# One slot in every 64 fetched by SyncE, row by row, in place of a GpSimd gather

## The chip, the cores and the metric

The kernel runs on one core of a Trainium2 chip. The metric is the device time of one execution in microseconds (us): the median of several timed runs. All inputs and outputs are in HBM.

## What is computed

A graph network over N = 6250 nodes with 128 features and E = 200000 edges, which are sorted by destination. Two attention layers and one message layer each read the row of every edge's source node:

```python
# attention layer (twice), heads H=8, C=16
xs = (x @ lin_w.T).reshape(N, H, C)
alpha = a_src[src] + a_dst[dst] + a_edge
alpha = leaky_relu(alpha); m = segment_max(alpha, dst)
alpha = exp(alpha - m[dst]); alpha /= segment_sum(alpha, dst)[dst]
out = segment_sum(xs[src] * alpha[..., None], dst)
...
# message layer
em = relu(layer_norm(concat([x[src], x[dst]]) @ msg_w + msg_b))
msgs = segment_sum(em * edge_weights[:, None], dst)
```

Everything else (projections, layer norms, the update at the end) works on nodes, not on edges, and is short.

## The kernel before

**Tiling.** The edges are cut into slots of 128 edges whose destinations lie in one block of 128 nodes. There are 1616 slots. Four slots (G = 4) make a visit, so there are 404 visits (VISITS), and eight visits (SPAN) make a group z of the softmax. An edge's source row is fetched from a table in HBM into a ring in SBUF. Such a fetch is an indirect DMA of GpSimd: one instruction for each slot, 128 rows at once, addressed by a column of the index tile `slot_src`.

**Stages.** There are three stages with such gathers, one after another, each over all visits. Pass 1 reads `rows1` (265 floats a row, 1060 bytes) into a ring of 5 visits. Pass 2 reads `rows2` (136 floats) into a ring of 24 visits. The message stage reads `msg_rows` (128 floats) into a ring of 4 visits, and fetches 1624 slots. Node work lies between the stages.

**Order in a pass.** Each engine has its own hand-written program over a counter t, and semaphores join them. In iteration t of a pass:

- GpSimd (`edge_rows_in`) gathers visit v once visit v - 5 of the ring is consumed (pass 1) and once PE has selected the destinations of visit v - 4 (LEAD).
- ACT (`edge_act`) copies the part xs of visit t out of the ring (pass 1 alone, L1163), then evacuates the transposed one-hot of visit t + 2 (L1169), then casts the one-hot of visit t - 15 (L1175), and then does its step of the softmax.
- PE selects destination rows of visit t + 1 (L1073) and scatters visit t - 16 (L1057 to L1060).
- DVE takes the scores of visit t from the ring (`edge_take`, L1280 to L1285), weights, makes the one-hots (L1249) and adds.

The softmax of group z runs in steps p = 0 to 7 at t = 8 + 8z + p. In pass 1 its step 2 ends with an ACT copy that signals `e2_out` (L1203), which is at t = 8z + 10; step 5 is ACT's exp (L1211); DVE signals `topped` in step 5 or so (L1362).

**SyncE's queue.** In a pass SyncE issues few transfers (`edge_side_loads`). For each z it waits for `topped` of z - 2, issues three small loads (L995, L997, L998; in pass 2 a fourth, L1000), and in pass 1 then waits for `e2_out` of group z - 1 and stores that tile (L1004). In the message stage it issues nothing until the very end.

Of the kernel before, what the change touches and what calls it, by code (L numbers as in the profile page):

```python
# [41 lines left out]
SPAN = 8  # L42
WS = SPAN * G
# [47 lines left out]
class Build:  # L91


    def __init__(self, nc, ctx):
# [4 lines left out]
        self.arrived_before = [0] * ROWS_MOST  # L99

# [79 lines left out]
def load(queue, relay, dst, src):  # L180

    relay.done(queue.dma_start(dst, src))
# [12 lines left out]
class Setup:  # L195
# [3 lines left out]
    def __init__(self, K, edges):  # L199
# [42 lines left out]
        self.dstf = K.sb("lane_keys", [P, SC, P])[:, :, :]  # L242
# [13 lines left out]
def prepare(K, D, edges):  # L256
# [10 lines left out]
    erows = Relay(K.arrived[ROWS_MOST - 1], 16)  # L267
# [106 lines left out]
    srcs.done(act.activation(T.srcf, T.erow[:, :, 0, :].bitcast(i32), ACT.Copy))  # L374
    turned = K.relay("slots_turned")
# [51 lines left out]
    for relay in (made, filled, cleared, fold, place, srcs, words, wts, turned, evacuated, copied, squared, multiplied, copied_a,  # L427
                  links_out, wt_out, sent, h0_out, keys_first):
        relay.after(pe, act, dve, sp)
# [235 lines left out]
def project(K, name, sources, width, evacuate):  # L665

    pe, act, dve = K.pe, K.act, K.dve  # L670
    transposed, copied = K.relay(name + "_transposed"), K.relay(name + "_copied")
    multiplied, evacuated = K.relay(name + "_multiplied"), K.relay(name + "_evacuated")
    units = [(b, k) for b in range(NB) for k in range(len(sources))]

    def transpose(q):
        b, k = units[q]
        if q >= 2:
            pe.wait_ge(copied.sem, q - 1)
        transposed.done(pe.transpose(K.ps[:, q % 2, 0:P], sources[k][0][:, b, :], K.ident[:, :]))
        act.wait_ge(transposed.sem, q + 1)  # L680
        if q >= 2:
            act.wait_ge(multiplied.sem, q - 1)
        copied.done(act.activation(K.xT[:, q % 2, :], K.ps[:, q % 2, 0:P], ACT.Copy))

    transpose(0)
    for q, (b, k) in enumerate(units):
        if q + 1 < len(units):
            transpose(q + 1)
        pe.wait_ge(copied.sem, q + 1)
        if k == 0 and b >= 2:  # L690
            pe.wait_ge(evacuated.sem, b - 1)
        multiplied.done(pe.matmul(K.ps[:, 2 + b % 2, 0:width], K.xT[:, q % 2, :], sources[k][1],
                                  start=k == 0, stop=k == len(sources) - 1))
        if k == len(sources) - 1:
            dve.wait_ge(multiplied.sem, q + 1)
            evacuated.done(evacuate(b, K.ps[:, 2 + b % 2, 0:width]))
# [26 lines left out]
class DmaEvent:  # L723


    def __init__(self, K, sems, each, before):
        self.K, self.sems, self.each, self.before = K, sems, 16 * each, before
# [4 lines left out]
    def wait(self, engine, i, v):  # L732
        self.K.loop_wait(engine, self.at(v), i, self.each, (v // U + 1) * self.each + self.before[v % U])
# [10 lines left out]
class Gather:  # L744


    def __init__(self, K, name, source, buffer, freed, extra):
        self.K, self.source, self.buffer, self.freed = K, source, buffer, freed
        self.arrived = DmaEvent(K, K.arrived, G, list(K.arrived_before))
        for u in range(U):  # L750
            K.arrived_before[u] += 16 * G * (TURNS + (1 if u < extra else 0))

    def emit(self, i, v):
# [3 lines left out]
        for j in range(G):  # L757
# [58 lines left out]

WITHIN = "a slot's block counts the 48 block starts passed, and moves by one at most from slot to slot"
# [42 lines left out]
class Pass:  # L860


    def __init__(self, K, layer):
# [52 lines left out]
        event = lambda what: K.sem(n + what)  # L916
        self.made, self.transposed, self.turned, self.selected = event("made"), event("transposed"), event("turned"), event("selected")
        self.consumed, self.xs_copied, self.cast, self.columns = event("consumed"), event("xs_copied"), event("cast"), event("columns")
# [1487 lines left out]
```

## Time and profile before

| What | us |
|---|---|
| Median of 3 timed runs | 8398.62 (8397.52 to 8403.86) |
| Span of the profiled execution, first to last instruction | 6747.1 |
| Pass 1, gathers, from about | 92 to 2132 |
| Pass 2, gathers, from about | 2315 to 4349 |
| Message stage, to about | 6600 |

Of the profiled execution only the span is given, and no time of its own; the median of the timed runs is 1651.5 us above that span. The profile shows nothing outside the span. All rows below belong to the span. The two passes and the message stage make up nearly all of it.

### The profile page before, as it was taken

The page shows a single profiled execution, that of the slowest core. Times are in us where ns is not written, and L with a number is a line of the kernel's source. Part 1 is how long each engine was busy: PE and PEld are TensorE (multiplying, and loading weights), DVE is VectorE, ACT ScalarE, POOL GpSimd, SP SyncE. Part 2 cuts the span into 40 slices and gives each one's busy share as a digit, 9 for nine tenths or more (in the row PEclk, how much of TensorE's full clock was granted, in tenths as well). Part 3 has the DMA queues.
Part 4 walks back from the last instruction along what each step waited for, and adds up shares of the span by engine and source line. Part 5 has one row for each costly group of instructions (what it writes and reads, how often), then busy time and mean ns, then how long its engine had stood idle before and what let it go on. Part 6 is the DMA issues. An engine that isn't in the chain of part 4 may idle for free. (4 is left out here: it accounts for less than half of the span.)

```text
span 6747.1 us, 141313 instructions
## 1 busy us (share of the span) xinstructions
PE 5205.8 (77%) x33770; PEld 4594.2 (68%) x33770; DVE 4667.0 (69%) x15724; ACT 3002.7 (45%) x10366; POOL 4638.6 (69%) x4899
## 2 busy tenths in 40 slices
PE   4888888888888289989898988866776667767664
PEld 4667667677766277878787877756666666666664
DVE  4777777777777656666666666566777777777777
ACT  2444444444443322222222222265666666666666
POOL 4777777777774277777777777506777777777771
PEclk6898998989998666666666666678999999999997
DMA  7544444444443422222222222232222222222222
GB/s 168 152 117 116 116 116 116 117 116 116 116 116 77 115 62 63 62 63 65 63 63 63 63 64 63 49 87 60 54 54 54 54 54 54 54 54 54 54 54 30
DMA packets 335610, 537.84 MB, mean 80 GB/s; under 512 B 105870, under 2 KB 223135, under 8 KB 334481
## 3 DMA queue, kind: packets, MB, share of 16 engines
q0 software_dynamic: 182080, 441.08, 26.1%
q1 hardware_dynamic: 143462, 83.65, 4.6%
q8 instruction: 357, 5.85, 0.4%
q10 hardware_dynamic: 9323, 4.08, 0.3%
q14 instruction: 388, 3.18, 0.2%
HBM read 491.47 MB, written 42.61 MB: 79 GB/s over the span
## 5 line engine op out<-in xcount | busy, mean ns | idle before, releaser
L976 POOL DMA_INDIRECT arena<-rows,slot_src x3232 | 3081.1, 953 | 1024.2 <-issue 910.8
L759 POOL DMA_INDIRECT arena<-msg_rows,slot_src x1624 | 1532.5, 944 | 494.7 <-issue 489.4
L2071 PE MATMUL psum<-arena 128*128 x3248 | 710.1, 303 | 585.7 <-DVE arena L2091 364.6
L1169 ACT ACTIVATE arena<-psum 128x512 f32<-128x512 bf16 x808 | 479.9, 594 | 1305.0 <-PE psum L1018 1294.5
L2071 PEld LDWEIGHTS psum<-arena 128*128 128x128 f32 x3248 | 526.8, 204 | 655.0 <-issue 654.7
L1305 DVE TENSOR_TENSOR arena<-arena,psum 128x290 f32 x1616 | 731.4, 453 | 323.3 <-DVE arena L1305 312.9
L1058 PE MATMUL psum<-arena 128*128 128x145 f32 x3232 | 954.5, 386 | 0.0
L1073 PE MATMUL psum<-arena 128*128 x3232 | 687.7, 343 | 262.8 <-DVE arena L1285 157.0
L1060 PE MATMUL psum<-arena 128*128 128x145 f32 x3232 | 881.7, 364 | 0.0
L1437 DVE TENSOR_TENSOR arena<-arena,psum 128x129 f32 x1616 | 468.8, 290 | 528.6 <-PE psum L2132 465.0
L1073 PEld LDWEIGHTS psum<-arena 128*128 128x128 f32 x3232 | 518.0, 211 | 393.3 <-issue 365.5
L1073 PE MATMUL psum<-a_src_a_dst,arena 128*128 x3232 | 637.8, 316 | 177.3 <-DVE arena L1285 138.4
L2078 ACT ACTIVATE arena<-psum 128x128 bf16<-128x128 f32 x1624 | 426.1, 277 | 772.6 <-PE psum L2073 772.3
L1073 PEld LDWEIGHTS psum<-a_src_a_dst,arena 128*128 128x128 f32 x3232 | 608.0, 269 | 231.1 <-issue 219.1
L1060 PEld LDWEIGHTS psum<-arena 128*128 128x128 f32 x3232 | 675.3, 250 | 10.5 <-issue 2.4
L1242 DVE TENSOR_TENSOR arena<-arena,psum 128x512 f32<-128x512 f32 x808 | 553.5, 685 | 180.9 <-PE psum L1060 177.8
L2073 PE MATMUL psum<-arena,ident 128*128 128x128 f32 x3248 | 675.7, 292 | 0.0
L1058 PEld LDWEIGHTS psum<-arena 128*128 128x128 f32 x3232 | 643.8, 247 | 44.6
L2091 DVE SCALAR_TENSOR_TENSOR arena<-psum,node_small,vectors 128x128 f32<-128x128 f32 x1620 | 561.0, 346 | 44.4 <-DVE node_small L2087 1.8
L1249 DVE TENSOR_TENSOR arena<-psum,slot_local_dst 128x512 bf16<-128x512 bf16 x808 | 551.7, 683 | 0.2
L1280 DVE CUSTOM_DVE_ANT_0 arena<-arena,psum 128x128 bf16<-128x128 f32 x1616 | 367.8, 282 | 253.4 <-DMA arena<-rows,slot_src 185.4
L2073 PEld LDWEIGHTS psum<-arena,ident 128*128 128x128 f32 x3248 | 536.8, 208 | 0.0
(361 smaller groups left out, 9250.5 us busy)
## 6 DMA issues: line engine op xcount, KB each, us to landing
arena<-rows,slot_src POOLq DMA_INDIRECT x3232
arena<-msg_rows,slot_src POOLq DMA_INDIRECT x1624
arena<-slot_keys SPq DMA_DIRECT2D x100, 128.0 KB
edge_alpha<-arena SPq DMA_DIRECT2D x50, 128.0 KB
arena<-edge_alpha SPq DMA_DIRECT2D x50, 128.0 KB
slot_keys<-lane_keys SPq DMA_DIRECT2D x24, 256.0 KB
arena<-rows SPq DMA_DIRECT2D x6, 1024.0 KB, 9.9
rows<-arena SPq DMA_DIRECT2D x4, 822.0 KB
```

What stands on the lines that cost most here:

```text
L759: pool.indirect_dma_start(out=self.buffer[:, v % U, j, :], out_offset=None, in_=self.source, in_offset=bass.IndirectOffsetOnAxis(ap=K.SRC[ ...
L976: pool.indirect_dma_start(out=E.rowbuf[:, r, j, :], out_offset=None, in_=E.source, in_offset=bass.IndirectOffsetOnAxis(ap=K.SRC[:, at:at + ...
L1058: pe.matmul(sums[:, 0:AW], E.onehotF[:, u % 2, 2 * k, :], E.rhs[:, u % 2, 2 * k, :], start=True, stop=False, skip_group_check=True)
L1060: pe.matmul(K.ps[:, 3 + k, bass.ds(step_in(word, k), AW)], E.onehotF[:, u % 2, 2 * k + 1, :], E.rhs[:, u % 2, 2 * k + 1, :], start=False, ...
L1073: return pe.matmul(E.psX[:, j, 0:E.dcol], E.onehotT[:, v % 2, j, :], rows_.rearrange("p b w -> p (b w)"), start=True, stop=True)
L1169: act.activation(E.onehotT[:, v % 2, :, :], E.psT, ACT.Copy).then_inc(E.turned, 1)
L1242: dve.tensor_tensor(by_head(E.rhs[:, u % 2, :, 0:F]), by_head(xs), w.unsqueeze(3).broadcast_to([P, G, H, C]), ALU.mult).then_inc(E.weighte ...
L1249: dve.tensor_tensor(E.onehot[:, v % ONEHOTS, :, :], E.iota.unsqueeze(1).broadcast_to([P, G, P]), K.DL[:, v * G:v * G + G].unsqueeze(2).bro ...
L1305: dve.tensor_tensor(row, row, E.psB(k), ALU.add).then_inc(E.added, 1)
L2071: pe.matmul(psH[b][:, j, :], onehotT[:, b, j, :], K.by_dst[:, bass.ds(blocks(v, j), 1), :].rearrange("p b w -> p (b w)"), start=True, stop ...
L2073: last = pe.matmul(psH[b][:, j, :], K.ident[:, :], rowbuf[:, b, j, :], start=False, stop=True)
L2091: last = dve.scalar_tensor_tensor(rhs[:, b, j, 0:F], psH[b][:, j, :], rstd[:, b, j:j + 1], K.vec["L1_gnn_msg_g"], ALU.mult, ALU.mult)
```

## The change

One slot of every 64 is taken from GpSimd: slot j = 0 of each visit v = 15, 31, 47 and so on to 399 (`ASIDE`), 25 visits; in pass 1 the first two are left as they were, so there are 23. SyncE fetches the 128 rows of such a slot with 128 transfers of one row each. It reads the indices eight at a time from SBUF into registers; for each row it computes the address and issues the transfer into a staging buffer of two slots (which lies in the `lane_keys` tile). ScalarE then copies the 128 staged rows into the ring, one iteration ahead of the visit's first reader, and all readers of such a visit wait for that copy too. In the passes SyncE issues 64 rows after its side loads of each z, and so a slot in two halves (z even, z odd). In the message stage it issues them all in one sequence. The list of indices is kept in HBM once, in the setup.

```diff
+EVERY = 2 * SPAN
+ASIDE = [v for v in range(EVERY - 1, VISITS, EVERY)]
+IDX = 8
...
+    def load_indices(self, n):
...
+        sp.dma_start(K.aside_idx[:, n % 2, :], K.aside_src[i % 2:i % 2 + 1, i // 2, :]).then_inc(K.aside_idx_in[n % 2], 16)
+
+    def gather(self, n, part, parts):
+        K, sp = self.K, self.K.sp
+        if part == 0:
+            if n == 0:
+                self.load_indices(0)
+            sp.wait_ge(K.aside_idx_in[n % 2], self.idx_landed[n])
+            if n + 1 < len(self.visits):
+                self.load_indices(n + 1)
+            at_least(sp, self.copied, n - 1)
+        for at in range(part * P // parts, (part + 1) * P // parts, IDX):
+            _, nodes = K.nc.values_load_multi_w_load_instructions(K.aside_idx[0:1, n % 2, at:at + IDX], engines=[ET.SP],
+                                                                  skip_runtime_bounds_check_because=NODES)
+            for k in range(IDX):
+                node = nodes[k].with_bounds(min_val=0, max_val=N - 1)
+                sp.dma_start(self.buffer[at + k:at + k + 1, n % 2, :], self.source[bass.ds(node, 1), :]
+                             ).then_inc(K.aside_in[n % IDX], 16)
+
+    def copy(self, n, to):
+        K, act = self.K, self.K.act
+        act.wait_ge(K.aside_in[n % IDX], self.landed[n])
+        act.activation(to, self.buffer[:, n % 2, :], ACT.Copy).then_inc(self.copied, 1)
...
     def wait_rows(self, engine, v):
         r = v % self.rows
-        engine.wait_ge(self.K.arrived[r], self.before[r] + (v // self.rows + 1) * 16 * G)
+        engine.wait_ge(self.K.arrived[r], self.before[r] + sum(16 * len(js) for js in self.by_pool[r:v + 1:self.rows]))
+        n = self.aside.of(v)
+        if n is not None:
+            engine.wait_ge(self.aside.copied, n + 1)
...
         r = v % E.rows
-        for j in range(G):
+        for j in E.by_pool[v]:
...
             sp.wait_ge(E.e2_out, z)
             sp.dma_start(K.edge2[z - 1, :, 0:w], E.e2[:, b, 0:w]).then_inc(E.kept[b], 16)
+        n = E.aside.of(z // 2 * EVERY + EVERY - 1)
+        if n is not None:
+            E.aside.gather(n, z % 2, 2)
...
     for t in range(-2, VISITS + 16):
+        n = E.aside.of(t + 1)
+        if n is not None:
+            at_least(act, E.consumed, t + 2 - E.rows)
+            if not E.first:
+                at_least(act, E.weighted, t + 2 - E.rows)
+            E.aside.copy(n, E.rowbuf[:, (t + 1) % E.rows, 0, :])
...
+    S.sent.after(sp)
+    for n in range(len(gather.aside.visits)):
+        gather.aside.gather(n, 0, 1)
...
+        n = gather.aside.of(i * U + v + 1)
+        if n is not None:
+            summed.wait(act, i, v + 1 - U)
+            gather.aside.copy(n, rowbuf[:, (v + 1) % U, 0, :])
```

SyncE's queue in pass 1, at two neighbouring z, before (L1004 is the store that waits for `e2_out`):

```order
L997 DMA arena<-slot_keys 128x1
L998 DMA arena<-chunk_links 1x66
L1004 DMA edge_alpha<-arena 128x256 [waits edge1_e2_out]
L995 DMA arena<-slot_keys 128x2x128 [waits edge1_topped]
L997 DMA arena<-slot_keys 128x1
```

and the same place now, for an odd z, where the second half of a slot begins (L1033 to L1042 are the lines L995 to L1004 of before; L710 reads eight indices, the ISA row computes an address, L714 fetches one row of `rows1`):

```order
L1033 DMA arena<-slot_keys 128x2x128 [waits edge1_topped]
L1035 DMA arena<-slot_keys 128x1
L1036 DMA arena<-chunk_links 1x66
L1042 DMA edge_alpha<-arena 128x256 [waits edge1_e2_out]
L710 TENSOR_LOAD aside_indices
L714 ISA
L714 DMA lane_keys<-rows 1x265
L714 ISA
L714 DMA lane_keys<-rows 1x265
```

Behind the last of these rows the pair of ISA and DMA goes on to 64 rows, with a L710 before every eight; then comes the next z's L1033. So 64 transfers now stand between a store and the next side loads, and behind the wait for `e2_out`.

ACT's program in pass 1 around the first visit taken aside (v = 47), now; L1258 is the exp (L1211 before), L1210 the copy of xs (L1163), L1216 the evacuation of the one-hot (L1169), and L721 is new:

```order
L1222 ACTIVATE arena<-arena 128x512 [waits edge1_scattered]
L1224 ACTIVATE arena<-arena 128x4x16 [waits edge1_wt_out]
L1258 ACTIVATE arena<-arena 128x256 [waits edge1_lowered]
L721 ACTIVATE arena<-lane_keys 128x265 [waits aside_rows_in0,edge1_consumed]
L1210 ACTIVATE arena<-arena 128x512 [waits edge1_weighted,rows_arrived1]
L1216 ACTIVATE arena<-psum 128x512 [waits edge1_selected,edge1_transposed]
```

The copy of visit 8z + 7 (z odd) stands at the head of iteration t = 8z + 6, behind the exp of the softmax and ahead of everything else that ACT does from there on. The `e2_out` for which SyncE waits before the second half is signalled at t = 8z + 2, three iterations and a softmax step earlier.

## Rows read from the trace of the kernel before

**Rows 1.** The page: busy time of each engine over the span.

```profile
span 6747.1 us, 141313 instructions
PE 5205.8 (77%) x33770; PEld 4594.2 (68%) x33770; DVE 4667.0 (69%) x15724; ACT 3002.7 (45%) x10366; POOL 4638.6 (69%) x4899
```

**Rows 2.** Windows in pass 1, pass 2, message stage: busy us (instructions), clock, DMA share, GB/s.

```profile
core 0: us, PE busy (x) PEld busy (x) DVE busy (x) ACT busy (x) POOL busy (x), PEclk, DMA share, GB/s
1000.00:1500.00 500.00, 423.74 (x2697) 354.10 (x2697) 394.97 (x1724) 220.15 (x552) 378.44 (x400) 0.91 0.43 116
3000.00:3500.00 500.00, 450.39 (x2515) 401.46 (x2514) 304.73 (x729) 143.67 (x363) 378.91 (x398) 0.66 0.27 63
5000.00:5500.00 500.00, 342.57 (x2808) 321.02 (x2807) 361.86 (x1129) 308.61 (x1400) 378.11 (x401) 0.96 0.21 54
```

**Rows 3.** Groups of instructions, POOL: busy us, mean ns, idle before, releasers.

```profile
L976 POOL DMA_INDIRECT arena<-rows,slot_src x3232 | 3081.1, 953 | 1024.2 <-issue 910.8 <-PE psum L1073 76.1 <-DMA rows<-arena 29.0
L759 POOL DMA_INDIRECT arena<-msg_rows,slot_src x1624 | 1532.5, 944 | 494.7 <-issue 489.4 <-PE psum L2073 5.2
```

**Rows 4.** Waits in pass 1, window 500 to 2000: us, times, longest.

```profile
DVE arena L1280 <- DMA arena<-rows,slot_src: 135.2, 131, 2.4
ACT arena L1163 <- DMA arena<-rows,slot_src: 127.9, 91, 3.1
```

**Rows 5.** Waits in pass 2, window 2500 to 4000.

```profile
DVE arena L1285 <- DMA arena<-rows,slot_src: 360.6, 250, 3.7
```

**Rows 6.** Waits in the message stage, window 4800 to 6400.

```profile
PE psum L2071 <- DMA arena<-msg_rows,slot_src: 134.3, 102, 2.5
```

**Rows 7.** Timeline of SyncE in pass 1: start us, us, instruction.

```profile
609.61 0.32 SPq L1004 DMA_DIRECT2D edge_alpha<-arena  x1
...
649.91 0.32 SPq L1004 DMA_DIRECT2D edge_alpha<-arena  x1
...
663.89 0.47 SPq L997 DMA_DIRECT2D arena<-slot_keys  x1
664.40 0.29 SPq L998 DMA_DIRECT2D arena<-chunk_links  x1
690.25 0.32 SPq L1004 DMA_DIRECT2D edge_alpha<-arena  x1
```

**Rows 8.** Timeline of ACT in pass 1.

```profile
649.50 0.38 ACT L1203 ACTIVATE arena<-psum 128x256 f32<-128x256 f32 x1 [0.48 <-PE psum L1120]
...
652.74 0.63 ACT L1163 ACTIVATE arena<-arena 128x512 f32<-128x512 f32 x1 [0.87 <-DMA arena<-rows,slot_src]
...
663.14 0.42 ACT L1211 ACTIVATE arena<-arena 128x256 f32<-128x256 f32 x1 [2.78 <-DVE arena L1360]
```

**Rows 9.** Timeline of SyncE in the setup: sixteen transfers of 4 short rows.

```profile
38.30 5.35 SPq L182 DMA_DIRECT2D arena<-in_L_gnn_enc_w_T  x16
```

**Rows 10.** Loads of registers and address arithmetic: ns min/median/max (L822 eight words, PE).

```profile
L822 PEldq TENSOR_LOAD <-slot_words x157: 587/590/1132, 120.2 to 6583.1; - x157
L1073 PEldq FUSED_REGOPS  x3232: 46/53/55, 121.2 to 4349.2; - x191
```

**Rows 11.** Timeline of POOL: last two gathers of visit 108.

```profile
648.55 0.95 POOL L976 DMA_INDIRECT arena<-rows,slot_src  x1 [0.30 <-issue]
649.80 0.94 POOL L976 DMA_INDIRECT arena<-rows,slot_src  x1 [0.30 <-issue]
```

**Rows 12.** Timeline of SyncE in pass 2.

```profile
2834.10 0.37 SPq L995 DMA_DIRECT2D arena<-slot_keys  x1
...
2835.37 0.32 SPq L1000 DMA_DIRECT2D arena<-edge_alpha  x1
```

**Rows 13.** Timeline of ACT in pass 2.

```profile
2874.14 0.42 ACT L1211 ACTIVATE arena<-arena 128x256 f32<-128x256 f32 x1 [2.28 <-DVE arena L1360]
```

**Rows 14.** Timeline of DVE, first visits of pass 1, rows already landed.

```profile
128.24 0.18 DVE L1285 TENSOR_TENSOR arena<-arena,psum 128x32 f32<-128x32 f32 x1
...
139.46 0.18 DVE L1285 TENSOR_TENSOR arena<-arena,psum 128x32 f32<-128x32 f32 x1
```

**Rows 15.** The page, DMA queues that fetch instructions: packets, MB, share.

```profile
q8 instruction: 357, 5.85, 0.4%
q14 instruction: 388, 3.18, 0.2%
```

More of the change, by code:

```diff
@@ L99, in __init__ @@
         self.arrived_before = [0] * ROWS_MOST
+        self.aside_in = [self.sem(f"aside_rows_in{u}") for u in range(IDX)]
+        self.aside_idx_in = [self.sem(f"aside_indices_in{u}") for u in range(2)]
+        self.aside_before, self.aside_idx_before = [0] * IDX, [0, 0]
     def sb(self, name, shape, dt=fp32):
@@ L374, in prepare @@
     srcs.done(act.activation(T.srcf, T.erow[:, :, 0, :].bitcast(i32), ACT.Copy))
+    erows.after(sp)
+    for k in range(2):
+        lane = (ASIDE[k] * G % P) // 2
+        load(sp, aside_out, K.aside_src[k:k + 1, :, :], T.erow[lane:lane + 1, :, 0, :].bitcast(i32))
     turned = K.relay("slots_turned")
@@ L662, in slots_each @@
     return min(WS, SLOTS - z * WS) // CH
[L665 to L696, printed above, removed]
@@ L720, in wait, with __init__ @@
         at_least(engine, self.sem, i * U + v + 1)
-class DmaEvent:
-    def __init__(self, K, sems, each, before):
-        self.K, self.sems, self.each, self.before = K, sems, 16 * each, before
+class RowsEvent:
+    def __init__(self, K, sems, before, aside):
+        self.K, self.sems, self.before, self.aside = K, sems, before, aside
+        self.by_pool = [range(G) if aside.of(g) is None else range(1, G) for g in range(VISITS + U)]
     def at(self, v):
@@ L732, in wait @@
     def wait(self, engine, i, v):
-        self.K.loop_wait(engine, self.at(v), i, self.each, (v // U + 1) * self.each + self.before[v % U])
+        g = i * U + v
+        engine.wait_ge(self.at(v), self.before[g % U] + 16 * sum(len(js) for js in self.by_pool[g % U:g + 1:U]))
+        n = self.aside.of(g)
+        if n is not None:
+            engine.wait_ge(self.aside.copied, n + 1)
 def slots_of(i, v):
@@ L814, in pieces @@
     return out
+NODES = "a slot's sources are nodes of the graph, 0 to N - 1, or the node 0 of a slot's filling"
 WITHIN = "a slot's block counts the 48 block starts passed, and moves by one at most from slot to slot"
@@ L928, in __init__ @@
         self.loaded = [K.sem(f"{n}marks_in{u}") for u in range(2)]
-        self.kept = [K.sem(f"{n}edge2_kept{u}") for u in range(2)]
+        self.kept = [K.sem(f"{n}edge2_kept{u}") for u in range(2)] if first else []
         self.each = 48 if first else 64
         self.before = list(K.arrived_before)
+        self.aside = Aside(K, f"edge{layer}", self.source, self.row, [v for v in ASIDE if not first or v >= 2 * EVERY])
+        self.by_pool = [range(G) if self.aside.of(v) is None else range(1, G) for v in range(VISITS)]
         for v in range(VISITS):
-            K.arrived_before[v % self.rows] += 16 * G
+            K.arrived_before[v % self.rows] += 16 * len(self.by_pool[v])
     def wait_rows(self, engine, v):
         r = v % self.rows
-        engine.wait_ge(self.K.arrived[r], self.before[r] + (v // self.rows + 1) * 16 * G)
+        engine.wait_ge(self.K.arrived[r], self.before[r] + sum(16 * len(js) for js in self.by_pool[r:v + 1:self.rows]))
+        n = self.aside.of(v)
+        if n is not None:
+            engine.wait_ge(self.aside.copied, n + 1)
     def wait_marks(self, engine, z):
```

42 lines of the change are left out of this document (31 added, 11 removed).

## The prediction

> **What bounds the kernel now.** I read the page first: no engine is busy over 77% of the span [rows 1], so the limit has to be found stage by stage. The windows by stage show one thing in common: in 500 us GpSimd issues 400 gathers in pass 1, 398 in pass 2 and 401 in the message stage [rows 2]. That is 1.25 us a gather, whatever the row length. Its groups say why: 0.95 us busy and 0.3 us of "issue" before each; over 3232 gathers of the passes it waited for another engine's work only 76.1 us (PE), and over 1624 of the message stage 5.2 us [rows 3]. So GpSimd sets the pace of all three stages, 5.0 us a visit, 80 us for 16 visits. The others wait for its rows: DVE 135.2 us of 1500 in pass 1 (9%), ACT 127.9 [rows 4]; DVE 360.6 of 1500 in pass 2 (24%) [rows 5]; PE 134.3 of 1600 in the message stage (8%) [rows 6]. The reader is to see two sizes here: fewer gathers are worth 1.25 us each, and in pass 1 the consumers have less than a tenth to spare.
>
> **What is removed.** 23 + 25 + 25 = 73 gathers of 1.25 us: 91 us, 1.4% of the span. The consumers of pass 2 (24% starved) and of the message stage (8%) can follow a pace 1.6% faster.
>
> **The price of a row on SyncE.** Per row there is one transfer, one address computation and an eighth of a register load. The nearest transfers: the one-piece load L998 takes 0.29 us, and L997 ahead of it ends 0.04 us before it starts [rows 7], so 0.33; sixteen short ones take 5.35 us, 0.334 each [rows 9]. None has its address in a register, which the trace does not show; I take 0.35, and as the dear bound L997 with its 128 pieces, 0.47 + 0.04 = 0.51 [rows 7]. The address: 53 ns on PE, with the gap 0.09 [rows 10]. The load of eight words: 0.59 + 0.04 us [rows 10], 0.08 a row. Sum 0.52 us a row, with the bounds 0.33 + 0.05 + 0.07 = 0.45 and 0.51 + 0.09 + 0.08 = 0.68; I stay near the lower, since the one-piece form is the row's own. Half a slot, 64 rows, is then 33.3 us and a whole one 66.6.
> The register load is where a rule speaks against the change. The row says 0.59 us for eight words on PE, 74 ns a word [rows 10]. The Trainium skill (Runtime: NRT & Kernel Launch, section Instruction fetch mechanics) gives about 200 ns a register even for bulk loads. By the row the sum is 0.52 us a transfer, by the page it would be 0.35 + 0.09 + 0.20 = 0.64.
>
> **Where those rows lie: pass 1.** Here is the step on which I rest the forecast. For odd z SyncE begins the second half only behind the store that waits for `e2_out`. ACT wants the slot at the head of iteration 8z + 6, behind its exp. In the trace the store goes out at 649.91 [rows 7] and ACT is through the exp at 663.14 + 0.42 = 663.56 [rows 8]: 13.7 us later. SyncE needs 0.36 for the store, 33.3 for the rows, and then the last must land: a gather that ended at 649.80 + 0.95 = 650.75 [rows 11] released ACT at 652.74 [rows 8], so 2.0 us. Together 35.7. ACT is held for 22.0 us once in 16 visits. Behind the held copy on ACT's queue stand the copies of xs, the evacuation of the one-hots, the casts for the scatter and the softmax; PE and DVE have about one visit of work left without them, so the whole pass stands.
> Can it be made up? GpSimd works on for some three visits (LEAD 4, ring of 5), so rows are ready when ACT goes on. Then the consumers set the pace, not GpSimd. Sixteen visits take 690.25 - 609.61 = 80.6 us [rows 7]; without the 13.7 there are 66.9 left, which include the starved 9% [rows 4]. I take nine tenths, 60.2 us. The new period is 35.7 + 60.2 = 95.9 us against 80.6, and the gathers of 63 slots (79) no longer show. Cost: 15.3 x 23 = +352 us; nothing of the 29 us removed here comes back. The first half (z even) is hidden: it takes 33.7 + 1.6 us for the store and side loads, in the 36.3 us (0.9 x 40.3) from one `e2_out` to the next.
>
> **Pass 2.** No store stands ahead: SyncE starts at `topped` with four side loads, from 2834.10 to 2835.37 + 0.32 [rows 12], 1.6 us with the gap. ACT is at the place of the copy at 2874.14 + 0.42 [rows 13], 40.5 us after. Needed: 1.6 + 33.3 + 2.0 = 36.9. It fits with 3.6 us to spare, up to a row of 0.57 us. Gain 25 x 1.25 = 31 us.
>
> **Message stage.** SyncE has nothing else to do and may be two slots ahead; 66.6 us a slot against 79. It fits up to a row of 0.61 us. Gain 31 us.
>
> **The rest.** ACT's copy of 265 columns costs less than the 0.63 us of the 512 columns of L1163 [rows 8]; ACT is busy 29 to 62% [rows 2], so 50 of the 73 copies cost nothing, and the 23 of pass 1 lie in the hold, at most 10 us, which I leave within the nine tenths. If that cover were gone it would be 0.4 us each, 30 us. The two stores of indices in the setup are about 1 us of SyncE beside slower work. No bytes are added: 128 rows move to another queue.
>
> **Sum.** +352 - 31 - 31 = +290 us on a span of 6747.1. The median of the timed runs is 8398.6, that is 1651.5 us above the span, and no row shows what lies there; I take it as constant. 8398.6 + 290 = 8689, said as 8690. A 0.2% difference, 17 us, is about what a measurement of this kernel can tell from no change.
>
> **Rivals.**
> 1. *A row costs 0.58 us or more, and SyncE becomes the bound of every stage.* For it: no row shows a transfer addressed by a register, and L997's form costs 0.51. Against: both one-piece forms agree on 0.33. Priced at 0.64: in pass 1 the first half with store and side loads takes 41.0 + 1.6 = 42.6, the second 41.0 + 2.4 = 43.4, and from the copy to the next `e2_out` 0.9 x 26.6 = 23.9, together 109.9, +29.3 x 23 = +674. Pass 2: 2 x 42.6 = 85.2 against 80.3, +122. Message stage: 81.9 against 80, +48. Sum +844: 9243. The page's 200 ns a register would give just this row.
> 2. *The part outside the span grows with the program.* It is 1651.5 us for 141313 instructions [rows 1], 11.7 ns each, and SyncE gets some 19900 more: +233, so 8923. For it: it is large, and nothing else on the page is so unusual. Against: the instructions are fetched inside the span, 9.03 MB by two queues [rows 15], at under 1% of the transfer engines' time.
> 3. *The other side: the hold is covered, and the kernel is faster.* If the 1651.5 us were instead a slower gather in unprofiled runs, 0.34 us on each of 4869, a gather would take 1.59 and 64 of them 102 us. The period of 95.9 then hides behind GpSimd, and 73 x 1.59 = 116 us are gained: 8283. It decides from 1.52 us a gather (95.9 / 63). Against: all 1.25 us intervals of the trace agree. A quicker consumer works to the same side: its first visits with rows landed go at (139.46 - 128.24) / 3 = 3.74 us [rows 14], but those have neither softmax nor scatter; at 3.74 the period is 35.7 + 50 = 85.7, total +55, and only together with the 0.45 us row does it come out faster.
> 4. *No change within 0.2%:* costs and gains meet, for which the hold would have to be about 4 us above the period of before.
>
> **How the numbers follow.** Forecast (hold in pass 1, the other two stages gain): 0.57, with a range of its own from 8465 (row 0.45, consumers at 0.85: period 31.2 + 56.9 = 88.1, +172 - 62 = +110, less some) to 8900 (row 0.58, hardly a gain in pass 2). Rival 1: 0.14. Rival 2: 0.11. Rival 3: 0.13. Rival 4: 0.05. The range 8450 to 9250 takes in the forecast and rivals 1 and 2 at their prices and leaves out 3 and 4. Faster 0.13, same 0.05, slower 0.82.
>
> **What would show it.** In the changed profile, pass 1: ACT's staged copy waits some 20 us for a SyncE transfer, 23 times, GpSimd waits for PE or ACT there, and pass 1 grows from 2040 to about 2390 us of gathers. Each row transfer starts 0.52 us after the last. In pass 2 and in the message stage the staged copy waits for nothing, GpSimd keeps 1.25 us a gather, and each stage is 31 us shorter. Wrong would be a row price over 0.57, a pass 1 that catches up between two holds, or a difference between median and span that moved.

## The result, and the profile after

| | before, us | changed, us | ratio |
|---|---|---|---|
| Median of 4 runs each | 8398.07 (8396.76 to 8403.86) | 9791.9 (9782.42 to 9803.89) | 1.1651 [1.1616, 1.1685] |

The changed kernel is 1394 us slower. The prediction said 8690, so +290, with 9250 as its upper end: the sign was right, the size far off.

One thing has to be said before any row is read. **The kernel before takes one of two times, depending on the chip it runs on**: 8380 to 8400 us on chips 5 and 8, and 6745 to 6756 us on chips 1, 2 and 14 (medians beside the experiments below). No chip showed both times. But chips 5 and 8 were used in one session each, both earlier than every session on chips 1, 2 and 14, so that the time belongs to the chip and not to the hour is inferred and not shown. The timed runs of the table are of the first kind, while the trace of [rows 1] to [rows 15], with its span of 6747.1 us, is of the second; on which chips these two were taken is not on record. Below, "the 8400 chips" and "the 6750 chips" are these two kinds. The profile after is from an 8400 chip: its execution took 9803.89 us and its span is 9802.1, so only 1.8 us lie outside it.

The page of the changed kernel, beside [rows 1] and [rows 15]:

```profile
span 9802.1 us, 170711 instructions
...
PE 5741.3 (59%) x33770; PEld 5096.4 (52%) x33770; DVE 4674.2 (48%) x15724; ACT 3012.2 (31%) x10439; POOL 4563.4 (47%) x4826
...
q14 instruction: 618, 5.06, 0.2%
```

Windows in the middle of pass 1, pass 2 and the message stage, beside [rows 2] (busy us and instructions by engine, granted clock, DMA share, GB/s):

```profile
1000.00:1500.00 500.00, 282.94 (x1598) 240.05 (x1598) 234.29 (x1025) 131.16 (x332) 224.73 (x237) 0.72 0.26 70
4500.00:5000.00 500.00, 326.14 (x1800) 289.92 (x1800) 218.20 (x523) 102.86 (x262) 265.10 (x279) 0.63 0.20 45
8000.00:8500.00 500.00, 277.19 (x1906) 258.50 (x1906) 248.67 (x775) 211.97 (x964) 256.40 (x272) 0.78 0.14 38
```

GpSimd issues 237, 279 and 272 gathers in 500 us, not the 400, 398 and 401 of [rows 2]. Part of that is the kind of chip: on an 8400 chip the kernel before itself issues 293, 326 and 328 (first experiment below). The new copy, L721, and the row transfers, L714, seen by line (ns as minimum, median and maximum):

```profile
L721 ACT ACTIVATE arena<-lane_keys x73: 309/316/424, 463.7 to 9644.1; 128x136 f32<-128x136 f32 x25, 128x128 f32<-128x128 f32 x25, 128x265 f32<-128x265 f32 x23
...
  DMA lane_keys<-rows: 1264.9, 48
  DMA lane_keys<-msg_rows: 542.3, 25
...
L714 SPq FUSED_REGOPS  x9344: 1/37/1394, 361.6 to 9642.8; - x199
L714 SPq MOVE lane_keys<-rows x6144: 2/29/1407, 361.7 to 6529.2; - x199
L714 SPq DMA_DIRECT2D lane_keys<-rows x6144: 2/225/1409, 361.7 to 6529.3; - x199
...
L714 SPq DMA_DIRECT2D lane_keys<-msg_rows x3200: 1/225/1397, 6773.4 to 9642.9; - x189
...
L710 SPq TENSOR_LOAD <-aside_indices x1168: 3/777/1016, 360.7 to 9639.0; - x195
```

Two things are to be seen. First, ScalarE waits for SyncE's rows at all 73 copies, 1264.9 + 542.3 = 1807.2 us; the prediction had 23 such waits. Second, by the medians a row costs what the prediction's sum said, but the maxima are far off: a MOVE of 29 ns can take 1.4 us. In the records of L714, 839 address computations, 979 MOVEs and 995 transfers of this trace last over 0.6 us. In the message stage SyncE issues without pause: 3200 rows from 6773.4 to 9642.9, 0.897 us a row, where undisturbed ones start 0.41 us apart and eight with their load take 4.11 us, 0.51 each.

The chain from that transfer to the other engines is in the waits. Window 500 to 3500, pass 1, of the changed kernel (us in total, times, longest), where [rows 4] had the DMA of the gathers as the largest:

```profile
POOL arena L1014 <- ACT arena L1210: 712.2, 66, 31.7
ACT arena L721 <- DMA lane_keys<-rows: 689.6, 22, 34.9
...
DVE arena L1327 <- ACT arena L721: 558.7, 22, 31.9
...
PE psum L1059 <- ACT arena L1216: 509.7, 22, 29.1
```

and window 7000 to 9500, the message stage, beside [rows 6]. Its largest wait in total, ACT's for a "remote" release (a semaphore update whose source the trace doesn't show), is of the kind that the kernel before has on an 8400 chip too; the ones below are new:

```profile
ACT arena L2132 <- remote: 906.2, 307, 3.2
...
ACT arena L721 <- DMA lane_keys<-msg_rows: 479.3, 22, 23.3
...
PE psum L2121 <- ACT arena L721: 453.3, 22, 22.2
POOL arena L790 <- PE psum L2123: 406.6, 22, 20.0
```

In the message stage ACT waits for the rows, PE for ACT, and GpSimd for PE: 22 times each in the window, about as long each time.

### The profile page after: what moved, and what is told of

It reads as the page before. It is cut to its first block and busy times, and to the rows that moved or that the text cites. A ratio compares the mean times of both kernels' runs of the same rounds, so it can differ in the third digit from the quotient of the medians.

```text
span 9802.1 us, 170711 instructions
## 1 busy us (share of the span) xinstructions
PE 5741.3 (59%) x33770; PEld 5096.4 (52%) x33770; DVE 4674.2 (48%) x15724; ACT 3012.2 (31%) x10439; POOL 4563.4 (47%) x4826
## 5 line engine op out<-in xcount | busy, mean ns | idle before, releaser
L1014 POOL DMA_INDIRECT arena<-rows,slot_src x3184 | 3027.8, 951 | 3230.0 <-PE psum L1114 1077.8
L790 POOL DMA_INDIRECT arena<-msg_rows,slot_src x1599 | 1510.6, 945 | 1380.0 <-remote 555.2
L1216 ACT ACTIVATE arena<-psum 128x512 f32<-128x512 bf16 x808 | 480.7, 595 | 2348.3 <-remote 1425.1
L1114 PE MATMUL psum<-arena 128*128 x3232 | 733.0, 368 | 713.8 <-DVE arena L1296 444.6
L2121 PE MATMUL psum<-arena 128*128 x3248 | 786.6, 328 | 529.7 <-ACT arena L721 512.6
L1099 PE MATMUL psum<-arena 128*128 128x145 f32 x3232 | 1058.7, 422 | 0.0
L1059 PE MATMUL psum<-ident_bf,arena 128*128 128x128 bf16 x3232 | 422.0, 272 | 987.9 <-ACT arena L1216 958.5
L1114 PEld LDWEIGHTS psum<-arena 128*128 128x128 f32 x3232 | 574.1, 240 | 817.6 <-issue 804.1
L2186 PE MATMUL psum<-arena 128*128 128x129 f32 x3232 | 561.9, 326 | 711.7 <-DVE arena L1484 502.7
L1101 PE MATMUL psum<-arena 128*128 128x145 f32 x3232 | 949.3, 388 | 0.0
L2121 PEld LDWEIGHTS psum<-arena 128*128 128x128 f32 x3248 | 614.5, 235 | 535.7 <-issue 535.5
L2186 PEld LDWEIGHTS psum<-arena 128*128 128x128 f32 x3232 | 476.4, 225 | 788.2 <-issue 670.4
L1059 PEld LDWEIGHTS psum<-ident_bf,arena 128*128 128x128 bf16 x3232 | 305.2, 124 | 1101.1 <-issue 1042.8
L1101 PEld LDWEIGHTS psum<-arena 128*128 128x128 f32 x3232 | 761.0, 278 | 4.4 <-issue 0.8
L1099 PEld LDWEIGHTS psum<-arena 128*128 128x128 f32 x3232 | 722.3, 276 | 62.9
L2123 PE MATMUL psum<-arena,ident 128*128 128x128 f32 x3248 | 749.8, 317 | 4.6 <-issue 2.0
```

The costliest lines, as they stand in the source:

```text
L790: pool.indirect_dma_start(out=self.buffer[:, v % U, j, :], out_offset=None, in_=self.source, in_offset=bass.IndirectOffsetOnAxis(ap=K.SRC[ ...
L1014: pool.indirect_dma_start(out=E.rowbuf[:, r, j, :], out_offset=None, in_=E.source, in_offset=bass.IndirectOffsetOnAxis(ap=K.SRC[:, at:at + ...
L1059: last = pe.transpose(E.psT[:, j, :], E.onehot[:, v % ONEHOTS, j, :], K.ident_bf[:, :])
L1099: pe.matmul(sums[:, 0:AW], E.onehotF[:, u % 2, 2 * k, :], E.rhs[:, u % 2, 2 * k, :], start=True, stop=False, skip_group_check=True)
L1101: pe.matmul(K.ps[:, 3 + k, bass.ds(step_in(word, k), AW)], E.onehotF[:, u % 2, 2 * k + 1, :], E.rhs[:, u % 2, 2 * k + 1, :], start=False, ...
L1114: return pe.matmul(E.psX[:, j, 0:E.dcol], E.onehotT[:, v % 2, j, :], rows_.rearrange("p b w -> p (b w)"), start=True, stop=True)
```

## The experiments

Each ran beside the kernel before on the same chip; "+" is against that. They are told by the question they answer.

**The kernel before again, and its trace (8400 chip).** No edit.

> The kernel before, unchanged, profiled once more: its timed runs stand 1651 us above the span of the trace that the prediction was read from, while the changed kernel's runs stand only 1.7 us above their spans. Theory A (that trace shows an execution like the timed ones, and a constant lies outside): the span is again near 6750 us. Theory B (the trace was of a quicker execution than the timed ones): the span is near 8396 us, and the trace shows where the 1650 us more are, by the granted clock of PE or by a slower GpSimd.

Measured: 8380.91 us, span 8379.1. So nothing lies outside the span. Its windows in the three stages, beside [rows 2]:

```profile
1000.00:1500.00 500.00, 353.18 (x1987) 300.02 (x1988) 295.68 (x1279) 160.52 (x408) 278.29 (x293) 0.76 0.31 86
4000.00:4500.00 500.00, 400.21 (x2054) 355.46 (x2053) 248.79 (x597) 118.13 (x297) 311.11 (x326) 0.63 0.20 52
7000.00:7500.00 500.00, 334.13 (x2316) 313.41 (x2314) 295.27 (x922) 253.74 (x1150) 309.57 (x328) 0.85 0.16 44
```

Its gathers in the passes, in the view of groups, beside [rows 3]:

```profile
L976 POOL DMA_INDIRECT arena<-rows,slot_src x3232 | 3087.1, 955 | 2192.4 <-issue 874.1 <-remote 597.3 <-PE psum L1073 563.7
```

PE's sequencer at L1073, seen by line, beside [rows 10]:

```profile
L1073 PEldq ALU_OP  x5656: 2/36/728, 118.6 to 5544.6; - x196
L1073 PEldq FUSED_REGOPS  x3232: 2/55/720, 118.7 to 5544.7; - x191
```

A gather still takes 0.955 us and its "issue" gap is no larger. What is new is waiting: 597.3 us until a "remote" release and 563.7 for PE, where [rows 3] had 76.1. GpSimd doesn't set the pace here; the consumers do. From its first to its last gather pass 1 takes 2771 us, pass 2 2486 and the message stage 2466, against 2040, 2034 and 2026 in the first trace: that is 1622 of the 1632 us between the two spans, so the difference lies in the stages. And single sequencer instructions reach 0.72 us, where [rows 10] had 55 ns as the maximum. Yet they are few on PE: 44 of its 18202 address and register instructions last over 0.6 us, 31 us together, so their own length doesn't make the 1632. What does grow is time in which PE, DVE and ACT all stand still for more than 1 us: 20 such stretches with 92 us in the first trace, 265 with 777 us here.

**The removal alone (8400 chip).** GpSimd skips the 73 slots, SyncE fetches nothing and nobody waits; the 73 slots hold stale rows.

```diff
     def gather(self, n, part, parts):
+        return
     def copy(self, n, to):
-        act.wait_ge(...); act.activation(...)
+        return
```

> GpSimd skips the 73 slots, and nobody fetches them: their part of the ring keeps an older visit's rows, so part of the input of those slots is stale. It gives what the removal alone is worth. If GpSimd's 1.25 us a gather sets the pace: 91 us below the kernel before. If in the timed state another engine sets the pace: no change.

Measured: 8284.45 us, ratio 0.987 [0.9821, 0.9918], -102 us. The 91 us of the prediction lie within the interval (69 to 150 us), but not for its reason: by the first and last gathers pass 1 is 68 us shorter, pass 2 3 us longer and the message stage 37 us shorter, where the prediction had 29, 31 and 31, each from GpSimd's pace. On this kind of chip the agreement of the sums is in part luck.

**The fetch beside (8400 chip).** GpSimd gathers all slots; SyncE issues its 9344 rows too, and nobody reads or waits for them.

```diff
-            at_least(sp, self.copied, n - 1)
+            if n >= 2: sp.wait_ge(K.aside_in[(n - 2) % IDX], self.landed[n - 2])
...
-        act.wait_ge(...); act.activation(...)
+        return
```

> GpSimd gathers all slots as before; SyncE issues all its 9344 row transfers too, into the staging buffer, and nobody reads or waits for them. If only the hold costs time (a wait of ACT for late rows), this runs within 1% of the kernel before. If the row transfers themselves slow other engines (contention for the transfer engines, for semaphores or for instruction fetch), it is slower by several hundred us.

Measured: 9336.1 us, ratio 1.1122 [1.1051, 1.1194], +949 us. I first read this as SyncE's rows slowing the other engines. The trace says otherwise. Seen by line, L715 are the rows and L790 the gathers of the message stage:

```profile
L715 SPq DMA_DIRECT2D lane_keys<-msg_rows x3200: 3/225/1388, 6277.9 to 9230.5; - x189
...
L790 POOL DMA_INDIRECT arena<-msg_rows,slot_src x1624: 938/944/961, 6280.1 to 8781.1; - x181
```

One of the larger waits in window 3400 to 5900, pass 2:

```profile
DVE arena L1362 <- DMA arena<-edge_alpha: 437.7, 42, 14.8
```

In the message stage SyncE issues without pause, 0.923 us a row, and GpSimd's gathers take 8781.1 - 6280.1 = 2501 us; in the kernel before on the same chip they take 8241.3 - 5775.2 = 2466. So rows of that density slow the others by 1.4%. The stage ends late all the same, because SyncE is not done until 9230.5. And in pass 2 DVE waits 437.7 us for a side load of SyncE's, which stands behind 64 rows. Both are the queue of SyncE, which is full: it spends 95, 95 and 99% of the three stages inside its rows. By stages, pass 1 takes 2911 us (2771 in the kernel before), pass 2 2825 (2486), and SyncE's tail behind the last gather is 449.

**When SyncE's instructions are long (the same trace, and that of the changed kernel).** Behind GpSimd's last gather at 8781.1 SyncE goes on issuing rows for 449 us. Seen by line, first the 448 us before that moment, then the 448 us behind it:

```profile
L715 SPq MOVE lane_keys<-msg_rows x422: 3/18/757, 8333.1 to 8780.2; - x141
...
L715 SPq MOVE lane_keys<-msg_rows x856: 14/29/38, 8783.1 to 9230.5; - x172
```

It issues 422 rows while GpSimd gathers, and 856 in the same time once it has stopped: 1.06 us a row against 0.52, the price of an undisturbed one. The changed kernel shows the same inside the message stage, where GpSimd stands for 19.84 us:

```profile
6999.93 0.94 POOL L790 DMA_INDIRECT arena<-msg_rows,slot_src  x1 [0.30 <-issue]
7020.72 0.94 POOL L790 DMA_INDIRECT arena<-msg_rows,slot_src  x1 [19.84 <-PE psum L2123]
...
L714 SPq MOVE lane_keys<-msg_rows x25: 29/29/38, 7002.4 to 7014.7; - x25
```

Counted over the 28032 address computations, MOVEs and transfers of L714 in the changed kernel:

| The instruction starts | count | of these over 0.6 us |
|---|---|---|
| while a gather runs | 12093 | 1615 (13%) |
| less than 1 us after a gather's end | 2852 | 1131 (40%) |
| 1 to 3 us after | 5740 | 67 (1%) |
| more than 3 us after | 7347 | 0 |

PE is not what matters: 1951 of the last 7347 start while a matmul runs. So on an 8400 chip a row is dear only beside GpSimd's gathers, or beside something that comes and goes with them. It is no matter of SyncE's own instruction stream, which is the same behind 8781.1. Why the same gathers disturb nothing on a 6750 chip is open.

**Only pass 1 left as it was (8400 chip).** The lane works in pass 2 and in the message stage.

```diff
-[v for v in ASIDE if not first or v >= 2 * EVERY]
+[v for v in ASIDE if not first]
```

> Slots are taken aside in pass 2 and the message stage alone. By my prediction's step (only pass 1 holds ACT) this would be 60 us faster than the kernel before. If late rows hold ACT in every stage (the changed kernel's trace shows 437 us of such waits in 2400 us of pass 2 and 479 in 2500 of the message stage), it is slower, by about the changed kernel's loss in these stages.

Measured: 9179.88 us, ratio 1.0936 [1.0884, 1.0989], +793 us. By the first and last gather of each stage, pass 1 takes 2774 us (2771 in the kernel before), pass 2 2845 (2486), the message stage 2889 (2466). The two stages in which I saw a gain lose 782 us, by themselves.

**What of the row costs SyncE's time (8400 chip).** Four kernels with the fetch beside, and cheaper rows: addresses that are constants; the first of each eight rows alone; eight neighbouring rows in one transfer; constants, and a whole piece in one transfer.

```diff
-            _, nodes = K.nc.values_load_multi_w_load_instructions(...)
-                node = nodes[k].with_bounds(min_val=0, max_val=N - 1)
+                node = (n * 997 + (at + k) * 61) % N            # fixed rows
...
-            for k in range(IDX):
+            for k in range(1):                                  # one in eight; with bass.ds(node, IDX): eight each
...
+                sp.dma_start(self.buffer[at:at + w, n % 2, :], self.source[at + n * 64:at + n * 64 + w, :]  # w = P // parts
```

> As the kernel with rows fetched beside (GpSimd gathers every slot, SyncE issues 9344 one-row transfers that nobody reads), but each row's address is a constant: no register load, no address computation, no MOVE, so one SyncE instruction a row in place of about three. The rows fetched are arbitrary ones; the output is computed from GpSimd's rows alone. With registers this cost +949 us. If the transfers themselves (their number and their semaphore updates) slow the other engines: +800 to +1000. If it is the number of SyncE's instructions: about a third, +300. If it is the eight-word register loads: about 0. My theory is the transfers: +850.

> As the kernel with rows fetched beside, all 1168 register loads of eight words kept, but only the first of each eight rows is fetched: 1168 transfers in place of 9344. Transfers or bytes as the cause: an eighth, +120. Instructions: about a sixth, +150. Register loads as the cause: +800 to +949. Expected +120.

> As the run with one row in eight, but each transfer fetches eight neighbouring rows of the table: 1168 transfers and the full 9344 rows. If the number of transfers or of instructions counts: the same as that run, +120 to +150. If the bytes or the number of rows written count: +800 to +949. Expected: the same as one row in eight, within 30 us.

> Fetched beside, but with fixed addresses and a whole piece in one transfer: two transfers of 64 rows a slot in the passes, one of 128 in the message stage, 123 in all, and no register at all. The bytes are those of the full fetch. All theories but bytes: within 20 us of the kernel before. Bytes: +800 to +949. Expected 0 to +20.

| Beside the kernel before | instructions added, nearly all SyncE's | us | ratio |
|---|---|---|---|
| 9344 rows, registers (above, chip 8; the others chip 5) | 29305 | +949 | 1.1122 [1.1051, 1.1194] |
| 9344 fixed rows | 9447 | +158 | 1.0188 [1.0161, 1.0214] |
| one row in eight | 4777 | +94 | 1.0111 [1.0081, 1.0142] |
| eight rows each | 4777 | +106 | 1.0131 [1.0104, 1.0159] |
| fixed, 123 transfers | 224 | +7 | 1.0003 [0.9971, 1.0034] |

My theory, that the number of transfers costs the time (+850 for the fixed rows), fell: the same 9344 transfers cost 158. Bytes fell too (eight rows each). A fixed row keeps SyncE for 24.4 / 64 = 0.38 us on average, so that a slot, 49 us, fits any stage. The cost is steep only where SyncE has no room left. What remains, 1.1 to 1.9% for 4777 to 9447 instructions, is not explained by a full queue, and I did not find its cause.

**Number of instructions, or their form.** Two plain semaphore updates ahead of each fixed row; three updates in place of each row and no transfer; and register-addressed rows whose registers are loaded and addresses computed only once a piece.

```diff
+                K.sp.nop(nofuse=True).then_inc(K.spare, 1)     # twice ahead of each fixed row; or three times, without the row
...
+            if at == part * P // parts:
                 _, nodes = K.nc.values_load_multi_w_load_instructions(...)
```

> As the run with fixed row addresses (9344 transfers whose address is a constant, +158 us), but with two plain semaphore updates on SyncE ahead of each transfer, so that SyncE runs three instructions a row as in the run with registers (+943 us), and none of them touches a register. The updated semaphore is read by nobody. If what slows the other engines is the number of instructions that SyncE is fed: +700 to +950. If it is the register-addressed form of the transfer or the address arithmetic: +158 to +250. I expect the number of instructions, +800.

> As the run before, but with no row transfers at all: SyncE runs three plain semaphore updates in place of each row, 28032 in all, and nobody waits for them. Nothing moves but instructions. Number of instructions as the cause: +600 to +900, no transfer being needed. Transfers or registers as the cause: 0 to +30. Expected +700.

> As the run with rows fetched beside (+949 us), all 9344 transfers with an address from a register, but the registers are loaded and the addresses computed only once a piece, eight of them, and used by all rows of the piece: 121 register loads in place of 1168 and 968 address computations in place of 9344. If the form of the transfer is the cause: +850 to +949. If the number of instructions: with transfer and MOVE left, two a row, +400 to +550. If address arithmetic or register loads: +158 to +250. Expected +450.

These fell on a 6750 chip (the kernel before 6755.59, 25 runs), and showed no difference, so the +800, +700 and +450 expected of them were not put to the test: ratios 1.0 [0.9991, 1.001], 1.0001 [0.9992, 1.0011] and 1.0 [0.999, 1.001]. Repeated on two more chips of that kind they did so again:

> 28032 plain semaphore updates on SyncE beside the kernel before, nothing else. Where the kernel before takes about 6755 us: no change, as measured. Where it takes about 8400 us: +600 to +900 if the number of instructions that SyncE is fed slows the others, 0 to +30 if it is transfers or registers. Expected there +700.

> 9344 fixed transfers and 18688 plain updates beside the kernel before. Where it takes about 6755 us: no change, as measured. Where it takes about 8400 us: +800 if the number of instructions counts, +158 to +250 if it is the register-addressed form or the address arithmetic.

> 28032 plain semaphore updates on SyncE beside the kernel before, nothing else. Where the kernel before takes about 6750 us: no change, as measured twice. Where it takes about 8400 us: +600 to +900 if the number of instructions counts, 0 to +30 if it is transfers or registers.

Ratios 1.0 [0.9991, 1.001], 1.0004 [0.9995, 1.0014], 1.0 [0.999, 1.001]. So on a 6750 chip up to 28132 more instructions on SyncE, or 9344 more transfers, cost nothing. What they do on an 8400 chip stays open. The full fetch beside was not run on a 6750 chip.

**The changed kernel on a 6750 chip.** No edit; the kernel before takes 6745.36 us there.

> The changed kernel again. Where the kernel before takes about 8400 us: 9790 again. Where it takes about 6755 us and instructions aren't late: 64 rows in 33 us as in the prediction, a hold of some 22 us at each of the 23 slots of pass 1, pass 2 and the message stage 31 us shorter each; the prediction's steps then give +352 - 62 = +290, so 7045. If pass 1 catches up between two holds: about 6700, as in the run with the earlier start (6674).

Measured: 6969.3 us, ratio 1.0334 [1.0317, 1.0352], +224 us. The rows, L714, and the wait before the copy L721, seen by line:

```profile
L714 SPq MOVE lane_keys<-rows x6144: 29/29/43, 295.7 to 4573.8; - x199
L714 SPq DMA_DIRECT2D lane_keys<-rows x6144: 224/225/525, 295.8 to 4573.9; - x199
...
  DMA lane_keys<-rows: 514.7, 23
```

The three stages in windows, beside [rows 2]:

```profile
1000.00:1500.00 500.00, 337.97 (x2269) 284.04 (x2270) 328.55 (x1460) 186.89 (x475) 317.50 (x333) 0.85 0.37 99
3000.00:3500.00 500.00, 444.55 (x2547) 395.58 (x2545) 312.10 (x746) 145.74 (x370) 379.01 (x398) 0.69 0.25 64
5000.00:5500.00 500.00, 362.81 (x2847) 338.65 (x2846) 365.74 (x1143) 315.22 (x1431) 378.08 (x401) 0.93 0.20 55
```

One period of pass 1 in it, on SyncE and on ACT (L1042 is the store behind `e2_out`, L1258 the exp, L721 the copy):

```profile
1259.36 0.33 SPq L1042 DMA_DIRECT2D edge_alpha<-arena  x1
1261.00 32.60 SPq L714 DMA_DIRECT2D lane_keys<-rows  x64
...
1271.85 0.42 ACT L1258 ACTIVATE arena<-arena 128x256 f32<-128x256 f32 x1 [2.78 <-DVE arena L1407]
1294.69 0.42 ACT L721 ACTIVATE arena<-lane_keys 128x265 f32<-128x265 f32 x1 [22.42 <-DMA lane_keys<-rows]
```

This is the picture that the prediction drew: no long MOVE, 64 rows in 32.60 us, ACT held for 22.42 us, 23 times and in pass 1 alone, GpSimd at 398 and 401 gathers in the other stages.

**Pass 1 issued one group earlier.** The changed kernel, whole, with SyncE's halves one z ahead of where they stood, so that the last row is issued tens of us before ACT wants it.

```diff
-        n = E.aside.of(z // 2 * EVERY + EVERY - 1)
+        y = z + 1 if E.first else z
+        n = E.aside.of(y // 2 * EVERY + EVERY - 1)
         if n is not None:
-            E.aside.gather(n, z % 2, 2)
+            E.aside.gather(n, y % 2, 2)
```

> The changed kernel with one edit: in pass 1 SyncE issues each half of a slot one group z earlier, so that ScalarE's copy comes some 90 us after the last row is issued. The computation is whole. In the changed kernel pass 1 took 607 us more than before, of which 141 are also there with rows fetched beside. If the rest, 466 us, is the hold of ScalarE behind the second half: 9792 - 466 = about 9330 us. If ScalarE's hold was only a symptom, as SyncE can't keep up anyway: over 9650. Expected 9350.

> The changed kernel with pass 1's halves issued one group z earlier. Where the kernel before takes about 6755 us: -81 us, as measured. Where it takes about 8400 us: if the 466 us of pass 1 that the fetch beside doesn't explain are ScalarE's hold, 9792 - 466 = about 9330; over 9650 if SyncE can't keep up anyway.

> The changed kernel with pass 1's halves issued one group z earlier, a third time. Where the kernel before takes about 6750 us: -82 us, as measured twice. Where it takes about 8400 us: about +940 (9330) if the 466 us of pass 1 that the fetch beside leaves unexplained are ScalarE's hold; over +1250 if SyncE can't keep up anyway.

All three fell on 6750 chips: 6674.12, 6662.82 and 6669.37 us, ratios 0.988 [0.9863, 0.9896], 0.9879 [0.9863, 0.9896] and 0.9876 [0.9859, 0.9892]: 81 to 85 us faster than the kernel before, and some 306 us faster than the changed kernel (6969.3 to 6662.82 on chip 14). Its windows, pass 1 to message stage:

```profile
1000.00:1500.00 500.00, 419.72 (x2726) 346.30 (x2726) 400.51 (x1748) 223.39 (x563) 378.71 (x399) 0.94 0.45 118
3000.00:3500.00 500.00, 445.65 (x2550) 394.42 (x2548) 312.17 (x743) 146.57 (x374) 379.58 (x396) 0.69 0.29 65
5000.00:5500.00 500.00, 352.13 (x2853) 329.36 (x2852) 367.19 (x1149) 316.04 (x1435) 378.04 (x401) 0.95 0.22 55
```

No copy of this kernel waits for a row. The place of the 64 rows in SyncE's queue was the whole loss on such a chip. What it does on an 8400 chip is not measured.

## Why the prediction was wrong

**The step that failed.** It is the sentence "the median of the timed runs is 8398.6, that is 1651.5 us above the span, and no row shows what lies there; I take it as constant". Nothing of that kind lies outside a span: 1.8 us do. The 1651.5 us are the same stages running slower on the chips where the runs were timed, and every other number of the prediction (1.25 us a gather as the pace, 0.52 us a row, 80.6 us a period) is of the other kind of chip. The two figures that didn't meet, 6747 and 8399, were the warning; I noted it, and built a sum across it. The term of the sum that this upset is the price of a row: 0.52 us predicted, 0.76, 0.85 and 0.88 on average in the three stages of the changed kernel. With it fell the two overlaps "It fits" of pass 2 and the message stage, -31 and -31 us predicted, +371 and +423 measured, and pass 1 cost +606 in place of +352.

**On a 6750 chip, the kind of the trace, the steps held.** The changed kernel there costs +224 us where they gave +290:

| Step | predicted | measured |
|---|---|---|
| 64 rows on SyncE | 33.3 us | 32.6 |
| store to copy, with landing | 35.7 us | 35.2, mean of 23 |
| hold of ACT | 22.0 us, 23 times | 22.4 (514.7 / 23) |
| period of 16 visits in pass 1 | 95.9 us | 92.6 |
| pass 1, first to last gather | +352 | +277 (2316.4 against 2039.6) |
| pass 2 | -31 | -30.4 |
| message stage | -31 | -30.3 |

The hold's size was right; the period was 3.3 us too long, because the consumers without a wait for rows run at 0.86 of their pace (57.4 of 66.9 us), not at nine tenths. That term was mis-sized by 75 us, 3.3 in each of 23 periods. The copies of the other two stages cost nothing, as taken. The 0.52 us of a row came out as 0.51, but its parts didn't, and that is luck: 0.28 for the transfer with its gap (taken as 0.35), 0.07 for the address (0.09), 0.10 for the eighth of a load (0.08), and 0.06 for a MOVE that the sum had not foreseen.

**On the chips of the timed runs, rival 1 took place.** It said that from 0.58 us a row SyncE becomes the bound of every stage. A row costs 0.51 us undisturbed there too, but on average 0.76 in pass 1, 0.85 in pass 2 and 0.88 in the message stage (48.9, 54.5 and 56.0 us for 64). With the formula of rival 1 a slot in pass 2 then takes 2 x 54.5 + 3.2 = 112 us; measured between two copies are 113.9, and 114.3 in the message stage, against about 98 for 16 visits in both in the kernel before (2486 and 2466 us for 404 and 406 visits). By the first and last gathers of each stage that comes to +371 and +423 us for 25 slots each. In pass 1 a slot takes 136.4 us against 109.7: the hold is there as well, 31.4 us each, because 64 rows now take 41 us behind the store; +606 us. The sum, 1400, leaves 23 of the 1423 us between the two spans. The rival had the chance 0.14 and a price of 9243, since its row cost 0.64; what made a row dearer is not what it named (the form of the transfer or the load), but long single instructions of any kind, all of them during GpSimd's gathers or within 3 us of one.

**The rule of the Trainium skill** ("Runtime: NRT & Kernel Launch", section Instruction fetch mechanics) that gives about 200 ns for each register loaded: the eight-word load on SyncE has the median 777 ns after, and 783 on the 6750 chip, 97 to 98 ns a word. The sum had taken 74 by PE's row, and 200 would be two times too dear. The time of 9243 that went with it was nearer to the result, but for another reason. The same section of the Trainium skill says that the cost of fetching instructions is mostly hidden; on the 6750 chips this agrees, as 28132 instructions more on SyncE cost nothing. On the 8400 chips no run separates fetching from the rest for the whole kernel.

**Rival 2** (the part outside grows with the program) falls with the part itself. It also counted 19900 added instructions, without the MOVEs; there are 29398. On the 8400 chips the losses of three runs above, divided by the instructions added, give 17 to 22 ns each, but no run shows that their number is the cause. **Rival 3** had the right premise, that the 1651.5 us are slower stages, and the wrong end: it let GpSimd be slower and SyncE not. GpSimd's gather is 1.25 us on either chip when nothing holds it; consumers and SyncE are what slows. **Removed work:** 91 us predicted, 102 measured alone, with another split over the stages.

**Of the signs named in advance,** "a row price over 0.57" and "a difference between median and span that moved" both came true (0.76 to 0.88; from 1651.5 to 1.8 us). "Pass 1 catches up" did not.

**What stays open:** why GpSimd's gathers, or what comes with them, make a MOVE or an address computation of 30 to 40 ns take 0.7 or 1.4 us on chips 5 and 8, and not in the traces of the others; what makes PE, DVE and ACT stand still together for the 1632 us of the kernel before, and whether the "remote" waits are the same thing; and whether the number or the form of SyncE's instructions makes the 1 to 2% that remain.

## What to carry to other kernels

When the profiled span and the timed median of one program don't meet, compare the execution's own time with its span before anything is added up: a "constant rest" that nothing shows was here another pace, and every margin has to be worked out at that pace too. A queue that issues hundreds of small register-addressed transfers needs more room than the 3.6 us in 40 that looked enough here: the price of a row moved by 50 to 70% from one kind of chip to the other, while one of 0.38 us in the same place never became the bound. And where a long burst must go onto a queue that also waits, put it a whole group ahead of its reader: on a 6750 chip the same 9344 transfers cost 224 us in one place and gained 82 in the other.

## What the runs showed of the hardware

- The same program takes 6745 to 6756 us on chips 1, 2 and 14 and 8380 to 8400 on chips 5 and 8, 24% apart, with medians within 0.3% in each group. The durations of gathers, ACT and DVE instructions agree (0.953 and 0.955 us a gather). What differs is sequencer instructions of 0.7 us, waits with no visible release, and stretches of over 1 us in which PE, DVE and ACT all stand (777 us in all against 92). The granted clock differs as well, 0.91, 0.66 and 0.96 against 0.76, 0.63 and 0.85 in the three stages; PE is idle longer there, and the rows don't tell which came first.
- On an 8400 chip, SyncE's instructions of 30 to 260 ns last over 0.6 us in 40% of the cases that start less than 1 us after a GpSimd gather, in 13% of those during one, and in none of 7347 that start more than 3 us after the last. A row costs 1.06 us just before GpSimd's last gather and 0.52 just behind it. On a 6750 chip none of 28032 is that long.
- A register-addressed one-row transfer is three instructions on SyncE, an address computation (37 ns), a MOVE (29) and the transfer (225), 0.51 us with its eighth of a load. With a constant address it is one, of 0.25 us, and with an address already in a register two, 0.34 us (21.6 us for 64).
- 9344 register-addressed one-row transfers, or 28032 semaphore updates, beside a kernel with four busy engines cost it nothing measurable on a 6750 chip.
